# A spectral attention block on one core: reordered Gram pieces, half sums, more places and another split of copies around the token mix

## What is computed

```
xc  = layer norm of x over its last axis
tok = instance norm of the 128 tokens
k, q = Fourier layers of tok (16 heads, 64 x 64), v likewise (128 x 128)
attn = softmax(q k^T / scale) v          per image and head, 32 x 32
attn = Fourier layer of attn (16 heads -> 1) ;  attn = instance_norm(attn + tok)
m    = instance_norm(attn)
m    = gelu(instance_norm(spectral(m)) + skip(m))
m    = instance_norm(spectral(m)) + skip(m)
x    = x + instance_norm(m) + attn
x    = x + FFN(layer norm(x)), FFN: product with W, batch norm, recurrence y = sigmoid(wx + y V^T) over the rows
```

## Time and profile before

| | us |
|---|---|
| runs shown (three) | 413.95, 421.74, 422.87 |
| their median | 421.74 |
| the profiled execution's own time | 414.69 |
| its span | 412.9 |
| TensorE, VectorE, ScalarE, GpSimd busy | 348.2, 330.1, 220.5, 210.6 |

### The profile page before, as it was taken

How to read it: one execution, slowest core, us unless ns; L and a number is a source line. 1 busy time by engine, 2 the same in 40 slices (tenths; PEclk the granted TensorE clock), 3 DMA queues, 4 the chain that set the end, 5 groups by cost and what they waited for, 6 DMA issues and landing times.

```text
span 412.9 us, 6935 instructions
## 1 busy us (share of the span) xinstructions
PE 348.2 (84%) x2311; PEld 258.3 (63%) x2311; DVE 330.1 (80%) x944; ACT 220.5 (53%) x465; POOL 210.6 (51%) x241
## 2 busy tenths in 40 slices
PE   0299989999897599989999948887888886999992
PEld 0199974969444599988798936854444442346661
DVE  2999773279987868639999597899999956779996
ACT  0498862442022288636656314658777676655551
POOL 1289980000000699399994222888878400799300
PEclk9999999699999599999999978989999999999997
DMA  8999998999915000038999872058587868999975
GB/s 213 243 291 318 289 284 211 221 222 322 409 52 203 3 0 2 2 46 109 154 110 175 102 96 31 0 156 234 199 233 206 217 198 243 295 290 310 315 221 156
DMA packets 96148, 76.16 MB, mean 184 GB/s; under 512 B 6176, under 2 KB 88528, under 8 KB 94064
## 3 DMA queue, kind: packets, MB, share of 16 engines
q1 hardware_dynamic: 76384, 67.02, 57.7%
q0 software_dynamic: 16512, 8.39, 16.7%
q10 hardware_dynamic: 3216, 0.30, 0.8%
HBM read 47.22 MB, written 25.33 MB: 176 GB/s over the span
## 4 chain that ended last, share of the span: by engine, by line
PE 37%; DVE 29%; POOL 12%; DMA 8%; issue 4%; ACTq 3%; ACT 3%; SPq 3%; DVEq 0%; POOLq 0%
PE PS L652 32%; POOL BIG L593 8%; DVE SML L1243 6%; DVE BIG L1384 5%; PE PS L656 4%; DVE BIG L1577 3%; SPq L519 3%; DMA BIG<-rs_rows 3%; DVE BIG L1594 3%; ACTq L1039 2%; POOL BIG L612 2%; DMA BIG<-BIG 2%; DMA BIG<-xn_rows 2%; DVE BIG L1476 1%; DMA rs_rows<-SML 1%
## 5 line engine op out<-in xcount | busy, mean ns | idle before, releaser
L652 PE MATMUL PS<-CST,BIG 128*128 128x128 f32 (+6 forms) x994 | 124.9, 315 | 12.1 <-ACT BIG L1044 4.7
L652 PEld LDWEIGHTS PS<-CST,BIG 128*128 128x128 f32 (+1 forms) x994 | 112.0, 196 | 27.9 <-DVE BIG L1577 8.3
L606 POOL COPY BIG<-BIG 128x512 f32<-128x512 f32 x24 | 30.4, 1320 | 77.8 <-DMA BIG<-xn_rows 74.7
L652 PE MATMUL PS<-BIG 128*128 128x128 f32 (+2 forms) x450 | 55.9, 375 | 3.1 <-DVE BIG L1384 2.6
L1243 DVE BATCH_NORM_STATS2 SML<-BIG 128x6 f32<-128x128 f32 x256 | 53.4, 279 | 5.6 <-DMA BIG<-in_x 4.3
L656 PEld LDWEIGHTS PS<-CST,BIG 128*128 128x128 f32 (+1 forms) x326 | 37.7, 136 | 26.7 <-issue 16.7
L652 PE MATMUL PS<-BIG,SML 128*128 128x512 f32 (+4 forms) x134 | 50.3, 588 | 1.5 <-DVE PS L1638 1.5
L652 PEld LDWEIGHTS PS<-BIG 128*128 128x128 f32 (+2 forms) x450 | 42.9, 175 | 13.8 <-issue 8.4
L656 PE MATMUL PS<-CST,BIG 128*128 128x128 f32 (+1 forms) x326 | 46.6, 277 | 1.9 <-ACT SML L410 1.4
L410 ACT ACTIVATE BIG<-PS 128x512 f32<-128x512 f32 (+3 forms) x59 | 32.2, 567 | 26.3 <-PE PS L652 21.4
L593 POOL TENSOR_SCALAR BIG<-BIG,SML 128x128 f32<-128x128 f32 x84 | 40.0, 490 | 9.5 <-DVE SML L1263 9.5
(11 more groups left out here) (218 smaller groups left out, 476.5 us busy)
## 6 DMA issues: line engine op xcount, KB each, us to landing
xn_rows<-BIG SPq DMA_DIRECT2D x8, 1024.0 KB, 9.2
BIG<-xn_rows SPq DMA_DIRECT2D x8, 1024.0 KB, 8.8
BIG<-in_x POOLq DMA_DIRECT2D x8, 1024.0 KB, 11.1
BIG<-rs_rows SPq DMA_DIRECT2D x8, 1024.0 KB, 6.0
x_rows<-BIG SPq DMA_DIRECT2D x8, 1024.0 KB, 8.8
BIG<-x_rows SPq DMA_DIRECT2D x16, 512.0 KB, 7.3
out_x<-BIG SPq DMA_DIRECT2D x32, 256.0 KB, 3.7
BIG<-wy_rows SPq DMA_DIRECT2D x16, 192.0 KB, 6.8
```

The source lines that it names most:

```text
L606: pool.tensor_copy(x_mix[:, g % MIX_RING], columns(g)).then_inc(S("x_mix_pool"), 1)
L652: return pe.matmul(o, l, rhs, start=start, stop=stop, **k)
```

## The change

Seven edits around the mix. (1) Gram pieces are dealt out again between half attentions: all of image 3's stand before the attention of group 2. (2) `ma` is added in two halves, the first after the first half attention of group 3, and ScalarE squares each half by itself; the k1 product moves before the last half attention. (3) Three more places for columns, at 2144 in BIG3 (where one of the products of group 3 lay), so eight; the last three groups use these three. (4) ScalarE copies groups 0, 1, 3, 7, 11, ... 31 (ten), GpSimd the other 22. (5) GpSimd starts only when `dg` is written. (6) The copy to `y_m` stands behind `acft`. (7) ScalarE's square of `zw` moves from group 6 to 14, its root `r1` from 14 to 17; the squares of `ma` go to `sq_dump`.

```diff
@@ -57,9 +57,9 @@
 LN_POOL_N = [sum(LN_POOL[:c]) // 4 for c in range(XC + 1)]
 LN_ACT_N = [4 * c - LN_POOL_N[c] for c in range(XC + 1)]
 LAG_P2, LAG_M2 = 5, 7
-MIX_RING = 5
+MIX_RING, MIX_MORE = 5, 3
 XN_OUT = 4 * ["xn_0_3"] + 2 * ["xn_4_5"] + 2 * ["xn_6_7"]
-MIX_ACT = 4
+MIX_ACT = [0, 1, *range(3, G4, 4)]
 
 XA_AFTER = {3: (0,), 11: (1,), 15: (2,), 23: (3,), 27: (4,), 31: (5, 6, 7)}
 
@@ -272,7 +272,22 @@
             return tile[:, a:a + 1536].rearrange("p (w k h) -> p w k h", k=3, h=MH)
 
 
-        x_mix = BIG3[:, 5632:5632 + 512 * MIX_RING].rearrange("t (k w h) -> t k w h", k=MIX_RING, h=H)
+        x_mix = [BIG3[:, a + 512 * k:a + 512 * k + 512].rearrange("t (w h) -> t w h", h=H)
+                 for a, n in ((5632, MIX_RING), (2144, MIX_MORE)) for k in range(n)]
+
+        def mix_place(g):
+
+
+            if g < G4 - MIX_MORE:
+                return g % len(x_mix), g + 1 - len(x_mix)
+            return g - (G4 - MIX_MORE), g + 1 - MIX_RING
+
+        def columns_of(g):
+            return x_mix[mix_place(g)[0]]
+
+        def mix_count(act, g):
+            return sum((n in MIX_ACT) == act for n in range(g + 1))
+
         zt = BIG3[0:64, 0:4096].rearrange("k (t p) -> k t p", p=32)
         ta1 = BIG3[:, 4096:8192].rearrange("k (g n) -> k g n", n=H)
         y_m = BIG3[:, 8192:9216]
@@ -599,11 +614,13 @@
 
             pool.wait_ge(S("prod"), 2 * NH)
             pool.wait_ge(S("xt_in"), 16 * XC)
+            pool.wait_ge(S("y_filled"), 2)
+            pool.wait_ge(S("dg"), 1)
             for g in range(32):
-                if g % MIX_ACT != MIX_ACT - 1:
-                    if g >= MIX_RING:
-                        pool.wait_ge(S("mix_filled"), g + 1 - MIX_RING)
-                    pool.tensor_copy(x_mix[:, g % MIX_RING], columns(g)).then_inc(S("x_mix_pool"), 1)
+                if g not in MIX_ACT:
+                    if mix_place(g)[1] > 0:
+                        pool.wait_ge(S("mix_filled"), mix_place(g)[1])
+                    pool.tensor_copy(columns_of(g), columns(g)).then_inc(S("x_mix_pool"), 1)
             pool.wait_ge(S("kap"), 1)
             pool.wait_ge(S("a0"), 32)
             pool.wait_ge(S("mix_filled"), 32)
@@ -761,31 +778,34 @@
             last.then_inc(S("pt_filled"), 1)
             gram(2, 14, 26)
             pe.wait_ge(S("prob_t"), 1)
-            attend(0).then_inc(S("prod_used"), 1)
+            attend(0, [0])
+            gram(2, 26, 32)
+            attend(0, [1]).then_inc(S("prod_used"), 1)
             pe.wait_ge(S("cbd"), 1)
             tr(PS[:, 6, 0:128], cbd).then_inc(S("c_filled"), 1)
-            gram(2, 26, 32)
-            gram(3, 0, 6)
-            attend(1).then_inc(S("prod_used"), 1)
+            gram(3, 0, 12)
+            attend(1, [0])
+            gram(3, 12, 20)
+            attend(1, [1]).then_inc(S("prod_used"), 1)
             pe.wait_ge(S("cft"), 1)
             tr(PS[:, 6, 128:256], cft).then_inc(S("cf_filled"), 1)
             for k in range(2):
                 last = mm(bank(k), cft, t0[:, 512 * k:512 * k + 512])
             last.then_inc(S("cx_filled"), 1)
-            gram(3, 6, 20)
+            gram(3, 20, 32)
             attend(2).then_inc(S("prod_used"), 1)
-            gram(3, 20, 32)
-            attend(3, [0])
             pe.wait_ge(S("gx"), 1)
             pe.wait_ge(S("cf"), 1)
             for b in range(NB):
                 tb = slice(TB * b, TB * b + TB)
                 last = mm(PS[tb, 6, 0:32], fold, gx[:, tb])
             last.then_inc(S("gf_filled"), 1)
-            attend(3, [1])
+            attend(3, [0])
             mm(PS[0:1, 7, 0:1], ones[0:1, 0:1], ones[0:1, 0:1]).then_inc(S("y_filled"), 1)
             pe.wait_ge(S("gf"), 1)
             mm(PS[:, 6, 256:384], cft, gf).then_inc(S("k1_filled"), 1)
+            attend(3, [1])
+            mm(PS[0:1, 7, 1:2], ones[0:1, 0:1], ones[0:1, 0:1]).then_inc(S("y_filled"), 1)
 
             pe.wait_ge(S("dg"), 1)
             mm(PS[:, 6, 384:512], ones, dg).then_inc(S("bc_filled"), 1)
@@ -813,12 +833,10 @@
             for g in range(32):
                 if g >= 4:
                     pe.wait_ge(S("a0"), g - 3)
-                if g % MIX_ACT == MIX_ACT - 1:
-                    pe.wait_ge(S("x_mix_act"), (g + 1) // MIX_ACT)
-                else:
-                    pe.wait_ge(S("x_mix_pool"), g + 1 - (g + 1) // MIX_ACT)
+                act = g in MIX_ACT
+                pe.wait_ge(S("x_mix_act" if act else "x_mix_pool"), mix_count(act, g))
                 for w in range(4):
-                    last = mm(PS[:, 4 + g % 4, 128 * w:128 * w + 128], x_mix[:, g % MIX_RING, w, :], acft)
+                    last = mm(PS[:, 4 + g % 4, 128 * w:128 * w + 128], columns_of(g)[:, w, :], acft)
                 last.then_inc(S("mix_filled"), 1)
                 if g == 3:
                     pe.wait_ge(S("kap_dg"), 1)
@@ -1097,28 +1115,34 @@
                 tb = slice(TB * b, TB * b + TB)
                 last = act.activation(gf[tb, tb], PS[tb, 6, 0:32], ACT.Copy)
             last.then_inc(S("gf"), 1)
-            act.wait_ge(S("ma"), 1)
-            act.activation(ztmp, ma, ACT.Square, accum_out=s("p_ma")).then_inc(S("p_ma"), 1)
 
             def mix_columns(g):
-                act.activation(x_mix[:, g % MIX_RING], columns(g), ACT.Copy).then_inc(S("x_mix_act"), 1)
+                act.activation(columns_of(g), columns(g), ACT.Copy).then_inc(S("x_mix_act"), 1)
 
             act.wait_ge(S("xt_in"), 16 * XC)
-            mix_columns(MIX_ACT - 1)
+            act.wait_ge(S("prod"), 2 * NH)
+            mix_columns(MIX_ACT[0])
+            act.wait_ge(S("p_cx"), 1)
+            for k in range(2):
+                half = slice(512 * k, 512 * k + 512)
+                act.wait_ge(S("ma"), k + 1)
+                act.activation(sq_dump[:, half], ma[:, half], ACT.Square, accum_out=s(f"p_ma{k}")).then_inc(S("p_ma"), 1)
             root(s("al"), s("rt"))
+            mix_columns(MIX_ACT[1])
+            mix_columns(MIX_ACT[2])
             root(s("rm"), s("rt"))
 
             for g in range(32):
-                if g == 6:
+                if g == 14:
                     act.wait_ge(S("zw"), 1)
                     act.activation(ztmp, zw, ACT.Square, accum_out=s("p_z1")).then_inc(S("p_z1"), 1)
-                if g == 14:
+                if g == 17:
                     root(s("r1"), s("rt"))
                 act.wait_ge(S("mix_filled"), g + 1)
                 act.activation(a0[:, :, 4 * g:4 * g + 4],
                                PS[:, 4 + g % 4, :].rearrange("h (w t) -> h t w", w=4), ACT.Copy).then_inc(S("a0"), 1)
-                if g % MIX_ACT == MIX_ACT - 1 and g + MIX_ACT < 32:
-                    mix_columns(g + MIX_ACT)
+                if g + 4 in MIX_ACT and g in MIX_ACT[2:]:
+                    mix_columns(g + 4)
             load_table(ACT.Gelu)
             empty(act, "ta1", 0, 8, move_ta(ta1, 0))
             for i in range(G4 + LAG_M2):
@@ -1410,7 +1434,8 @@
             products(2)
             products(3)
             dve.wait_ge(S("y_filled"), 1)
-            TT(ma, cx, y_ps, ALU.add).then_inc(S("ma"), 1)
+            dve.wait_ge(S("prod"), 2 * NH)
+            TT(ma[:, 0:512], cx[:, 0:512], bank(2), ALU.add).then_inc(S("ma"), 1)
             dve.wait_ge(S("cf"), 1)
             dve.wait_ge(S("k1_filled"), 1)
             link(TT(k1x, PS[:, 6, 256:384], cf, ALU.mult))
@@ -1418,16 +1443,20 @@
             link(TS(s("q"), s("q"), 1.0 / PIX, None, ALU.mult))
             dve.wait_ge(S("p_cx"), 1)
             link(STT(s("q"), s("p_cx"), -2.0, s("q"), ALU.mult, ALU.add))
-            dve.wait_ge(S("ma"), 1)
+            dve.wait_ge(S("y_filled"), 2)
+            TT(ma[:, 512:1024], cx[:, 512:1024], bank(3), ALU.add).then_inc(S("ma"), 1)
             dve.wait_ge(S("p_ma"), 1)
-            link(STT(s("va"), s("p_ma"), 2.0, s("q"), ALU.mult, ALU.add))
+            link(STT(s("q"), s("p_ma0"), 2.0, s("q"), ALU.mult, ALU.add))
+            dve.wait_ge(S("ma"), 2)
+            dve.wait_ge(S("p_ma"), 2)
+            link(STT(s("va"), s("p_ma1"), 2.0, s("q"), ALU.mult, ALU.add))
             inv_root(s("al"), s("va"), EPS, prm("attn_norm_g"))
             TS(dg, ident, s("al"), None, ALU.mult).then_inc(S("dg"), 1)
-            link(dve.tensor_copy(y_m, y_ps))
             link(TT(s("x0"), s("al"), s("al"), ALU.mult))
             link(TT(s("x0"), s("x0"), s("va"), ALU.mult))
             dve.wait_ge(S("bc_filled"), 1)
             TT(acft, cft, PS[:, 6, 384:512], ALU.mult).then_inc(S("acft"), 1)
+            link(dve.tensor_copy(y_m, y_ps))
             inv_root(s("rm"), s("x0"), EPS, prm("norm2_g"))
             link(TT(s("kappa"), s("rm"), prm("mixer_skip_w1"), ALU.mult))
             TS(dg, ident, s("kappa"), None, ALU.mult).then_inc(S("kap_dg"), 1)
```

## The result

| | before | after |
|---|---|---|
| runs | 12 | 12 |
| median us | 416.44 | 412.28 |
| lowest to highest | 413.95 to 422.87 | 410.69 to 415.39 |
| profiled execution, its span | 414.69, 412.9 | 415.39, 412.3 |

The ratio of after to before is 0.9923, with a 95% interval of 0.9896 to 0.995: some 3.2 us faster (2.1 to 4.3 by the interval), a real difference but less than 2%. The profiled execution of after happens to be the slowest of its twelve, so its span must not be set against the span of before; its stages can be.

What follows compares the result with a forecast made beforehand. It took the last x_t load, ScalarE's copy behind it and then TensorE's mix to bound the kernel. Mix start -2.4 and later stall +0.9 made -1.5 us, from 418.3 to 416.8; range 409.7 to 421.4.

Steps and rivals of the forecast that it cites:

- rival 1: Mix: the clock doesn't stay down, or GpSimd's lock doesn't bite; -3.8 us, 414.5 us; chance 0.2.
- Gram pieces, +1.26: Ahead of group 1's second half attention: 14 more Gram pieces delay it and VectorE's products behind it by 1.26 us.
- No load last: Before the mix: Gram(3) ends earlier, x_t lands near 128 instead of 134.57, so products, not a load, come last.
- Halves, -0.99: Sum ma before the mix: halving saves 0.53 us on VectorE's add and 0.46 on ScalarE's square.
- Root not behind a copy, -0.94: Norm's chain before the mix: ScalarE copies group 0 earlier, so the root no longer waits behind a copy; -0.94 us.
- GpSimd held, -1.33: VectorE's two operations up to dg run without GpSimd's copies beside them; -0.61 and -0.72 us.
- y_m, -0.4: From dg to acft: with the y_m copy behind acft, 1.56 us become about 1.15; 0.2 saved by the lock rule.
- Start of the mix, -2.4: Sum to the first mix matmul: it starts 2.4 us earlier, near 137.3, bounds -1.4 to -3.2.
- What holds the mix up, +0.9: End of the mix: z3_1 comes later, behind root r1, and stalls TensorE's first transposes 0.3 to 1.5 us.
- The clock, 0: Start of the mix: TensorE's clock falls to half and returns as before, worth nothing either way.
- Rival 2: TensorE before its first transposes: late z3_1 stalls it 4.0 us and turns the sign, +1.6, 419.9 us; chance 0.17.
- Rival 3: Before the mix: the front gives nothing, Gram pieces cost 2.5 us or loads stay last; 418.3 us; chance 0.13.

Runs made afterwards that it cites:

- e7: Kernel after with the copy of y to y_m put back between dg and acft; no ratio, median 421.5 us of 4, last product to mix start 9.01 us.
- e11: Kernel after with five places for columns instead of eight; no ratio, median 419.82 us of 4, mix 35.73 us.
- e1: Kernel after run again with no edit; ratio to before 0.9898, last product to mix start 6.72 us, mix 36.05 us.
- e6: Kernel after with ma added in one operation and squared in one; ratio to before 0.9876, last product to mix start 7.37 us.
- e12: e5 plus three matmuls with unread results behind the last attention, to keep TensorE busy; ratio to before 0.9841, mix 34.39 us.
- e2: Kernel after with all Gram pieces beyond the old twelve moved behind the cx matmuls; ratio to before 0.9874, last product to mix start 6.42 us.
- e3: Kernel after with the old order of Gram pieces and of group 3's first half attention; ratio to before 1.0033, last product to mix start 10.54 us.
- e8: Kernel after with GpSimd not waiting for dg; ratio to before 0.9933, last product to mix start 7.66 us.
- e9: Kernel after with ScalarE's square of zw back before group 6 and root r1 before 14; ratio to before 1.0129, mix 41.73 us.
- e10: Kernel after with ScalarE copying only groups 3, 7, 11 and so on, GpSimd 24; no ratio, median 419.2 us of 4, mix 36.05 us.
- e5: Kernel after with VectorE making group 2's products before it waits for and copies cf; ratio to before 0.9862, last product to mix start 6.41 us.

## Why the prediction was right, and where its steps were off

The forecast of -1.5 us had the sign and the place; the ratio says -3.2, outside the forecast's own -0.5 to -2.5 and close to rival 1's -3.8, though not by rival 1's mechanism. The measured median, 412.28, lies in the wide range from 409.7 to 421.4. The 416.8 rested on an average of four executions that stood high; the median of before settled at 416.44 over twelve. Three of my signs were met in part by luck: the copy of cf at 116.98 (forecast 116.7), the first mix matmul at 137.89 (137.3) and the mix end at 172.93 (173) all hold 1.2 us by which the modes landed later in the profile of after. And I took the time outside the span to stay at 1.8 us; it grew to about 2.9.

*Gram pieces, +1.26: measured +0.35 where TensorE was on time, +1.75 to +2.34 where it was not.* This is the term that was mis-sized, and one profile couldn't show it. I counted from Gram(2) at 100.17 in the profile of before, where TensorE was late by a clock dip. Before, then after:

```profile
75.00:77.00 2.00, 2.00 (x10) 1.78 (x10) 0.37 (x4) 2.00 (x8) 0.00 (x0) 0.50 1.06 230
```

```profile
75.00:77.00 2.00, 2.00 (x21) 2.00 (x20) 1.03 (x5) 1.99 (x7) 0.00 (x0) 1.00 1.04 221
```

At 0.50 the 28 records of the low Gram product took 5.93 us, at 1.00 3.58. The same dip, with 5.50 to 5.96 us for these records, stands in the profiles of e7 to e11 and not in those of after, e1 to e6 and e12: six profiles of fourteen. TensorE's transposes of the probabilities stand at 99.5 to 101.8 with it and at 96.4 to 98.0 without. What it costs is read from the stretch between the start of the six products and the last product, in which none of these kernels differs from the kernel after except for the Gram order of e2 and e3:

| Gram order | without the dip | with the dip |
|---|---|---|
| old up to the copy of cf | 31.27 (e2), 31.26 (e3) | 31.27 (before) |
| of the change | 31.62 (after), 31.64 (e1), 31.61 (e6) | 33.02 (e8), 33.09 (e9), 33.61 (e7, e10, e11) |

The old order hid a late TensorE in the one profile of it that has the dip, the new one didn't in any of five: there the copy of cf waits for its transpose.

```profile
117.39 0.29 DVE L1432 COPY BIG<-PS 128x128 f32<-128x128 f32 x1 [3.77 <-PE PS L672]
```

That is e8, 3.77 us of wait against 2.38 in after and 2.02 before. In e8 TensorE reached the Gram pieces 1.82 us behind the start of the six products, as late as in the profile of before (1.83), and the order cost 1.75; in e7, e10 and e11 it was 2.41 behind and the order cost 2.34. So for the execution that I counted from my 1.26 was too small by 0.5, not too large: from the transpose of cbd to that of cft I had 8.22 us, and e8 shows 8.63 (108.40 to 117.03), which is 0.4 of the 0.5. The +0.35 of the profile of after is the price of an execution without the dip. How many of the twelve executions had it, the record doesn't say. The sum of the stages has to be read with this: where the dip comes, 1.0 to 1.6 are left of the 3.35 saved between P and the mix. Whether e5 and e12, where VectorE no longer waits there, would hide a dip was not seen; neither profile has one.

*No load last.* Right, and more than right: e3 shows that, with the copy of group 0 ahead of the squares, all the rest is worth nothing without it. I had booked the Gram order as a cost with a by-product.

*Halves, -0.99: -0.62* by the stages (0.65 by e6). The add's -0.53 holds. The square's term of -0.46 was the wrong one: 0.34 of it went into a longer pause between the accumulator read and VectorE's sum.

*Root not behind a copy, -0.94: -0.88. GpSimd held, -1.33: -1.33* in the stage; e8 gives 0.94, as then dg alone is met. Both right.

*y_m, -0.4: -0.59.* The lock that I let weigh in didn't bite: both tiny products were through before GpSimd's first copy. Where it does bite (e7), they took 1.06 and 0.94, about one GpSimd copy (1.06 alone). The Trainium skill, "SBUF — State Buffer", section "SBUF: two separate sides", says that a VectorE operation with two SBUF inputs and a GpSimd copy take a shared pair of ports for the whole instruction, so that the later one waits it out; the traces agree. GpSimd's copy to copy time is 1.0 to 1.41 us here.

*Start of the mix, -2.4: -3.0* (+0.35 - 3.35), inside the bounds given.

*What holds the mix up, +0.9: at most +0.1 in the profile of after, 0.65 in its repeat.* In after, root r1 moved by 3.0 us against the mix start (16.37 to 19.37), a little less than the 3.2 to 4.4 that I had, and the product behind its reciprocal took 0.38, not 1.01. z3_1 came 24.78 us after the mix start and just as it was wanted, with a gap of 0.08 in the weight loads. In e1, the same kernel, the root came at 19.63, that product took 1.10, z3_1 came 25.79 after the mix start, and TensorE waited 0.65; in e8 it waited 0.47, with 0.95 for the product. So "meeting within a microsecond" and a stall of 0.3 to 1.5 were right in mechanism, and the stall's absence in after is luck: 0.72 of the 1.01 between the two profiles is that one product beside GpSimd, 0.26 the root. There was no wait for kap_dg (4.0 after the start).

*The clock, 0.* It was low for 4.6 us of the mix, from 137.89 to about 142.5, against 4.8. In e2 and e5 it came back 4.1 us into the mix, and the mix was 0.6 shorter; in e8 after 5.2, and it was 0.9 longer. So the mix's length scatters by over a microsecond, with when the clock returns and with the wait for z3_1. Rival 1's gain from a clock that stays up isn't there even when it does stay up (e12). Rival 2, a z3_1 so late that the sign turns, did not happen, but e9 shows its mechanism: ScalarE's order in the mix can cost 6.7 us. Rival 3 is e3: had the load stayed last, there would have been no gain. Its other condition, Gram pieces at 2.5, is nearly met in e7, e10 and e11 (2.34).

What stays open is how much of the scatter of the kernel before (413.95 to 422.87, after 410.69 to 415.39) was the landing of the last load on its path; no run measured the landing by itself. Open too are the cause of the dip and of the 1.1 us more outside the span.

## What to carry to other kernels

Work that another engine's load waits for is to be placed by when the load must land, not only by what it costs where it stands: 14 Gram pieces moved ahead cost 0.35 us with TensorE on time and kept a load off a path on which it would have cost 3.8. But what such work costs depends on slack that one profile doesn't show. The same 14 pieces cost 1.8 to 2.3 us in the executions in which a clock dip 25 us earlier had made TensorE late, and the old order hid that dip in the one profile that shows it. Before a term is counted, look at several executions and check in each whether the engine was on time. And where VectorE and GpSimd share a stretch, short VectorE steps with two inputs in SBUF belong before GpSimd's first copy, since each one behind it can cost a whole copy.

## What the runs showed of the hardware that I had not expected

A one-column VectorE product takes 0.16 us alone and beside GpSimd's copies anything from 0.19 to 1.10, mostly 0.94 or more; a reciprocal or a product with a constant kept its 0.15 to 0.16 there. Strided products of 512 columns took 2.0 us instead of 1.1 when GpSimd got a copy in between (three of four in the profiles of after, e5 and e9), while before, back to back, they took 1.1 and GpSimd's copy waited 4.1. TensorE's clock dropped around 73 us, in a stretch where it was busy with short gaps only, in six of fourteen profiles, and not in the others of the same work. And keeping it at 2.4 GHz at the start of the mix with three matmuls is possible at no cost in the chain (P to mix 6.42 against 6.41), but worth only 0.1 us while GpSimd feeds TensorE.
